# A two-layer adjacency network on one core: exponentials ahead of the ramps, x added in the second layer, the weight splits moved off GpSimd, the packed codes three tiles ahead

## What is computed

```python
# layer 0: h = relu(layernorm(x)); two attention steps with the same mask
def _gat_layer(h, adj_mask, W_l, lw, lb, a):
    Wh = h @ W_l
    L1, L2 = (lw[:C], lw[C:])
    u = Wh @ L1 @ a
    v = Wh @ L2 @ a
    c = lb @ a
    e = jax.nn.leaky_relu(u + v.T + c, negative_slope=ALPHA)
    scores = jnp.where(adj_mask, e, NEG_INF)
    att = jax.nn.softmax(scores, axis=1)
    return jax.nn.elu(att @ Wh)
h = ALPHA * x + (1.0 - ALPHA) * _gat_layer(h, mask, W[i], lin_w[i], lin_b[i], attn[i])   # i = 0, 1
x = x + concatenate([h0, h1, h2]) @ mlp_w + mlp_b
# layer 1: h = relu(layernorm(x))
a = (adj == 1); x1 = a @ h / sum(a, axis=1)
x = x + concatenate([x1, h]) @ weight + bias
```

## Time and profile before

| what | value |
|---|---|
| median of 3 runs | 1790.13 us (1787.9 to 1791.51) |
| the profiled execution, its own time | 1792.32 us |
| its span, first to last instruction | 1790.5 us |
| busy: PE, DVE, ACT, POOL | 1545.7, 1565.8, 1249.3, 144.9 us |
| mean granted TensorE clock | 0.962 of full |
| HBM read and written | 323.35 MB and 27.33 MB |

### The profile page before, as it was taken

The page is one execution under the profiler, slowest core; times in us unless marked ns, Lnnn a source line. Parts: engine busy times, 40 slices in busy tenths (PEclk is TensorE's granted clock), DMA queues, the critical chain, the costliest instruction groups (busy, mean ns, idle before and its releaser), DMA issues. The chain is left out here.

```text
span 1790.5 us, 50269 instructions
## 1 busy us (share of the span) xinstructions
PE 1545.7 (86%) x21779; PEld 1495.5 (84%) x21779; DVE 1565.8 (87%) x2551; ACT 1249.3 (70%) x1341; POOL 144.9 (8%) x164
## 2 busy tenths in 40 slices
PE   2247698888888888888959999999999999799998
PEld 1237688788787878887849999999999999799998
DVE  7689999999999999999989859688696888986675
ACT  3266589898888888888768999999999996000000
POOL 1370000010101010101051000000000000000000
PEclk9668999999999999999979999999999999999999
DMA  7938899999999999999311111111211211133231
GB/s 243 239 144 307 337 362 389 373 380 391 376 405 361 407 367 404 360 407 356 151 43 45 56 44 49 39 59 43 61 55 37 60 31 43 54 102 96 84 96 49
DMA packets 114238, 353.93 MB, mean 198 GB/s; under 512 B 9056, under 2 KB 17248, under 8 KB 114016
## 3 DMA queue, kind: packets, MB, share of 16 engines
q1 hardware_dynamic: 92064, 304.50, 45.5%
q0 software_dynamic: 8512, 27.33, 5.7%
q10 hardware_dynamic: 13440, 18.88, 2.9%
HBM read 323.35 MB, written 27.33 MB: 196 GB/s over the span
## 5 line engine op out<-in xcount | busy, mean ns | idle before, releaser
L475 ACT ACTIVATE region<-ub,bigv 128x1024 uint8<-128x1024 f32 x1024 | 1099.3, 1150 | 81.1 <-DMA x_d<-region 30.9
L1445 PE MATMUL bank<-wsplit,region 128*128 128x195 bf16 x8192 | 791.0, 250 | 62.6 <-DVE region L791 53.8
L1445 PEld LDWEIGHTS bank<-wsplit,region 128*128 128x128 fp8e3 x8192 | 696.6, 99 | 76.4 <-DVE region L791 40.5
L1451 PE MATMUL bank<-wsplit,region 128*128 128x130 f16 x8192 | 558.3, 221 | 58.2 <-DVE region L799 56.9
L1451 PEld LDWEIGHTS bank<-wsplit,region 128*128 128x128 fp8e3 x8192 | 500.5, 98 | 87.7 <-DVE region L799 87.4
L799 DVE SCALAR_TENSOR_TENSOR region<-region 128x512 uint32<-128x512 uint32 x512 | 346.0, 694 | 21.7 <-PE bank L1451 21.0
L791 DVE SCALAR_TENSOR_TENSOR region<-region 128x512 uint32<-128x512 uint32 x512 | 343.1, 699 | 1.4 <-ACT region L475 1.3
L811 DVE TENSOR_SCALAR region<-region 128x4096 uint8<-128x4096 int32 x128 | 293.4, 2292 | 0.1
L1660 PE MATMUL bank<-wsplit,region 128*128 128x129 f16 x4096 | 243.3, 222 | 11.1 <-DVE region L1277 11.1
L1660 PEld LDWEIGHTS bank<-wsplit,region 128*128 128x128 fp8e3 x4096 | 241.0, 99 | 12.6 <-DVE region L1277 12.6
L1277 DVE TENSOR_SCALAR region<-region 128x512 uint32<-128x512 uint32 x256 | 100.4, 424 | 42.7 <-PE bank L1660 37.6
(11 more groups left out here) (183 smaller groups left out, 742.8 us busy)
## 6 DMA issues: line engine op xcount, KB each, us to landing
region<-in_adj SPq DMA_DIRECT2D x128, 2048.0 KB, 11.0
region<-codes_d SPq DMA_DIRECT2D x128, 256.0 KB, 2.7
codes_d<-region ACTq DMA_DIRECT2D x64, 256.0 KB, 6.3
ub<-u_d POOLq DMA_DIRECT2D x16, 512.0 KB, 5.8
hg<-h_d POOLq DMA_DIRECT2D x16, 256.0 KB, 4.8
region<-in_x SPq DMA_DIRECT2D x4, 512.0 KB, 6.3
h_d<-wsplit POOLq DMA_DIRECT2D x4, 512.0 KB, 4.3
x_d<-region POOLq DMA_DIRECT2D x8, 256.0 KB, 16.0
```

Source lines behind the costliest of these rows:

```text
L475: last = nc.scalar.activation(sv[:, b, :], ub[G % 2][:, :], ACT.Relu, bias=bigv[l][:, t:t + 1], scale=BIG)
L1445: return nc.tensor.matmul(acc_on[it], columns(onb[U % NS], it, b), wsplit[:, c * TC + 2 * q + b, 0:WC], start=(c == 0 and q == 0 and b == ...
L1451: return nc.tensor.matmul(acc_off[it], columns(offb[U % NO], it, b), woff[:, c * TC + 2 * q + b, WO:WO + WF], start=(c == 0 and q == 0 and ...
```

## The change

1. ScalarE runs `exps(0)` before any ramp of layer 0. The sum with x is no longer made at the start: L631 goes, ScalarE instead writes the MLP product alone (`m0`) next to hw. It lies over the last two on-buffers and the off-buffers, so the first ramps do not wait for its stores, but ramp 6 and the first off-mask do. The eight stores go out from SyncE's queue, between the loads of `adj`. x is read again in layer 1, and `old_x` has one addition more.
2. `split_off` and GpSimd's part go. Blocks 0 of both layers, and block 1 of layer 1, are split wholly on VectorE (`split`, 8 instructions). The other blocks are made by 5 VectorE instructions (`split_scaled`, `split_rest`, `split_last`) and 3 ScalarE casts (`cast_high`, `cast_middle`), spread over the tile ahead.
3. Codes are packed three tiles ahead instead of two, with four code buffers, and the second pair is packed in place in the strided `code` buffer.
4. The weights that the attention vectors don't need are loaded from ScalarE's queue, and VectorE and TensorE start on the six that they do need.
5. At the end of layer 0 `columns_out` of the last group but one and the third on-mask stand later in VectorE's order.

```diff
-NA, NP, NS, NO = 3, 3, 8, 6
+NA, NP, NS, NO = 3, 4, 8, 6
...
-        highp = at(58 * KB, 2 * KB, U8)
-        xb = [packed, highp]
-        pt = [at(60 * KB + 2 * i * KB, 2 * KB, U8) for i in range(NP)]
+        pt = [at(58 * KB + 2 * i * KB, 2 * KB, U8) for i in range(NP)]
...
-        xr = at(66 * KB, 16 * KB, FP32).rearrange("p (t c) -> p t c", c=C)
+        xq = [at(78 * KB + 4 * ((k + 1) % 4) * KB, 4 * KB, FP32).rearrange("p (t c) -> p t c", c=C) for k in range(4)]
+        m0 = [at(78 * KB + 2 * ((k + 2) % 8) * KB, 2 * KB, FP32).rearrange("p (t c) -> p t c", c=C) for k in range(NG)]
...
+        STORES = {3: (0,), 4: (1, 2), 5: (3,), 6: (4, 5, 6, 7)}
+
+        def nth(l, c):
+
+            return c if l == 0 else NCH - 2 + c
 
...
                     if m >= NA:
                         sp.wait_ge(coded, m - NA + 1)
                     sp.dma_start(adjb[m % NA], adj_v[g, h, :, :, c * CHJ:(c + 1) * CHJ]).then_inc(adj_in[m % NA], 16)
+                    for k in STORES.get(m, ()):
+                        sp.wait_ge(mm_out, 3 * k + 3)
+                        sp.dma_start(dgrp(m0_d, k), m0[k]).then_inc(m0_st, 16)
...
-                def split_off(l, c):
...
-                    ch.step(nc.gpsimd.tensor_tensor(po[:, 0:n, :], hw[:, ts, :], expv[:, ts, 1:2].to_broadcast([P, n, CE]), ALU.mult))
-                    ch.step(nc.gpsimd.tensor_copy(hi, po[:, 0:n, :]))
-                    nc.gpsimd.tensor_tensor(lo, po[:, 0:n, :], hi, ALU.subtract).then_inc(w_off, 1)
-                    pool.wait_ge(w_off, NCH * l + c + 1)
...
-                    pool.wait_ge(x0_r, 3 * k + 3)
-                    pool.dma_start(dgrp(x0_d, k), xr[:, grp(k), :]).then_inc(x0_st, 16)
...
                         pool.wait_ge(xm_r, e)
-                    pool.dma_start(xg[0], dgrp(x0_d, e)).then_inc(xg_in[0], 16)
+                    pool.dma_start(pairs(xi[e % 2]), xin_v[e]).then_inc(xi_in[e % 2], 16)
...
-                        nc.scalar.activation(hw[:, t0:t0 + nt, 0:C], pv[:, :, 0:C], ACT.Copy, scale=winv).then_inc(mm_out, 1)
+                        nc.scalar.activation(hw[:, t0:t0 + nt, 0:C], pv[:, :, 0:C], ACT.Copy, scale=winv)
+                        nc.scalar.activation(m0[X][:, 3 * r:3 * r + nt, :], pv[:, :, C + 2:], ACT.Copy, scale=winv).then_inc(mm_out, 1)
...
-                    elif U == 0:
-                        act.wait_ge(x0_st, 16 * NG)
+                    elif U == NS - 2:
+                        act.wait_ge(m0_st, 16 * NG)
...
+                def cast_high(l, c):
+                    act.wait_ge(sp_a, 2 * nth(l, c))
+                    nc.scalar.activation(wsplit[:, grp(c), 0:CE], av[:, :, :], ACT.Copy)
+                    nc.scalar.activation(woff[:, grp(c), WO:WO + CE], po[:, :, :], ACT.Copy).then_inc(sp_h, 1)
+
+                def cast_middle(l, c):
+                    act.wait_ge(sp_b, nth(l, c))
+                    nc.scalar.activation(wsplit[:, grp(c), CE:2 * CE], bb[:, :, :], ACT.Copy).then_inc(sp_m, 1)
...
+                    rows = slice(C * hf, C * (hf + 1))
+                    act.dma_start(wcat[rows, 0:3 * HC].rearrange("c (l x) -> c l x", x=HC)[:, :, C + 2:HC],
...
+                act.dma_start(mlpb[:, :], mlp_b.partition_broadcast(P)).then_inc(wts, 16)
+                act.dma_start(b1b[:, :], bias1.partition_broadcast(P)).then_inc(wts, 16)
...
                             products(k - 1, r, bank[3 * ((k - 1) % 2) + r])
-                ramps(0, 0, 0)
+                take_codes(0)
+                store_codes(0)
                 exps(0)
...
                     g, r = n // NCH, n % NCH
-                    if n > 0:
-                        ramps(0, n, 0)
+                    ramps(0, n, 0)
+                    if g == 0 and r > 0:
+                        cast_high(0, r)
                     ramps(0, n, 1)
-                    take_codes(n)
+                    if n + 1 < NT:
+                        take_codes(n + 1)
                     if r == 5 and g > 0:
                         high(NG + g - 1)
                     ramps(0, n, 2)
-                    store_codes(n)
+                    if n + 1 < NT:
+                        store_codes(n + 1)
+                    if g == 0 and r > 0:
+                        cast_middle(0, r)
                     ramps(0, n, 3)
                     if g > 0 and r == 7:
...
+                        if g == 0 and r > 1 and q == 0:
+                            cast_high(1, r)
+                        if g == 0 and r > 1 and q == 2:
+                            cast_middle(1, r)
...
                                             ALU.mult).then_inc(u_r, 1)
-                    nc.vector.scalar_tensor_tensor(xr[:, t0:t0 + nt, :], pv[:, :, C + 2:], winv, xr[:, t0:t0 + nt, :],
...
-                def split_on(l, c):
+                def split(l, c):
...
+                    sc.mark(nc.vector.tensor_tensor(full, hw[:, ts, :], expv[:, ts, 0:1].to_broadcast([P, n, CE]), ALU.mult))
+                    sc.mark(nc.vector.tensor_tensor(small, hw[:, ts, :], expv[:, ts, 1:2].to_broadcast([P, n, CE]), ALU.mult))
+                    sc.sync()
+                    sc.mark(nc.vector.tensor_copy(part[0], full))
+                    sc.mark(nc.vector.tensor_copy(hi, small))
+                    sc.sync()
+                    sc.mark(nc.vector.tensor_tensor(rest, full, part[0], ALU.subtract))
+                    nc.vector.tensor_tensor(lo, small, hi, ALU.subtract).then_inc(w_off, 1)
+                    sc.sync()
                     sc.step(nc.vector.tensor_copy(part[1], rest))
                     nc.vector.tensor_tensor(part[2], rest, part[1], ALU.subtract).then_inc(w_on, 1)
...
+                def split_scaled(l, c):
+                    dve.wait_ge(w_on, NCH * l + c)
+                    dve.wait_ge(w_off, NCH * l + c)
+                    nc.vector.tensor_tensor(av[:, :, :], hw[:, grp(c), :], expv[:, grp(c), 0:1].to_broadcast([P, IT, CE]), ALU.mult).then_inc(sp_a, 1)
+                    nc.vector.tensor_tensor(po[:, :, :], hw[:, grp(c), :], expv[:, grp(c), 1:2].to_broadcast([P, IT, CE]), ALU.mult).then_inc(sp_a, 1)
+
+                def split_rest(l, c):
+                    dve.wait_ge(sp_h, nth(l, c))
+                    nc.vector.tensor_tensor(bb[:, :, :], av[:, :, :], wsplit[:, grp(c), 0:CE], ALU.subtract).then_inc(sp_b, 1)
+                    nc.vector.tensor_tensor(woff[:, grp(c), WO + CE:WO + WF], po[:, :, :], woff[:, grp(c), WO:WO + CE],
+                                            ALU.subtract).then_inc(w_off, 1)
+
+                def split_last(l, c):
+                    dve.wait_ge(sp_m, nth(l, c))
+                    nc.vector.tensor_tensor(wsplit[:, grp(c), 2 * CE:WC], bb[:, :, :], wsplit[:, grp(c), CE:2 * CE],
+                                            ALU.subtract).then_inc(w_on, 1)
 
...
+                    elif U == 0:
+                        dve.wait_ge(m0_st, 16 * NG)
...
                     if n > 0:
-                        dve.wait_ge(pairs_r, 2 * n)
+                        dve.wait_ge(packed_r, n)
...
                     nc.vector.scalar_tensor_tensor(pk, cq[1], 2, cq[0], ALU.logical_shift_left, ALU.bitwise_or).then_inc(pairs_r, 1)
-                    nc.vector.scalar_tensor_tensor(hp, cq[3], 2, cq[2], ALU.logical_shift_left, ALU.bitwise_or).then_inc(pairs_r, 1)
+                    nc.vector.scalar_tensor_tensor(cq[2], cq[3], 2, cq[2], ALU.logical_shift_left, ALU.bitwise_or).then_inc(pairs_r, 1)
 
...
+                    nc.vector.scalar_tensor_tensor(pk, cq[2], 4, pk, ALU.logical_shift_left, ALU.bitwise_or).then_inc(packed_r, 1)
 
...
+                    if k == 4:
+                        convert(1, 0)
                     if k == 5:
-                        convert(1, 0)
+                        convert(1, 1)
                 biased_0()
                 largest_0(NG - 1)
                 max_parts(0)
-                convert(1, 1)
                 max_row(1)
                 pack_pairs(1)
                 max_out(1, hmx[:, 1, :])
                 scales(0)
                 pack(1)
+                convert(2, 0)
                 scales_end(0)
                 split_first(0)
-                split_on(0, 0)
+                split(0, 0)
+                convert(2, 1)
+                pack_pairs(2)
+                pack(2)
...
-                    ahead = n + 2 < NT
+                    ahead = n + 3 < NT
                     dve.wait_ge(p_in, n + 1)
+                    if n + 1 < NCH:
+                        split_scaled(0, n + 1)
                     on_mask(0, n, 0)
                     on_mask(0, n, 1)
                     off_mask(0, n, 0)
+                    if n + 1 < NCH:
+                        split_rest(0, n + 1)
                     if ahead:
-                        convert(n + 2, 0)
...
-                        split_on(0, r + 1)
+                        pack(n + 3)
+                    if n + 1 < NCH:
+                        split_last(0, n + 1)
...
-                columns_out(NG + e - 1)
```

(21 more changed lines are left out.)

97 lines of the change are left out of this document (40 added, 57 removed).

## The result

| | kernel before | changed kernel |
|---|---|---|
| median of 4 runs, us | 1789.59 (1787.9 to 1791.51) | 1757.6 (1757.12 to 1758.86) |
| profiled execution: span, own time, us | 1790.5, 1792.3 | 1755.5, 1757.3 |

A forecast was written before the change was run, and what follows sets the result against it. VectorE was taken to bound layer 0's middle, TensorE 950.2 to 1521.9, VectorE again to 1584.0. Terms 27.6 + 1.6 + 0.7 + 7 - 0.7 = 36.2 us off 1792.3 gave 1756.1, less 2.2 us 1753.9, so 1754; range 1743 to 1770.

The forecast's parts named there:

- Before the first off-mask: Start of layer 0: first off-mask at 90.5 instead of 104.3, set by the last store of m0; 13.8 us gained.
- Tiles 0 and 1: First off-mask to tile 2's first on-mask: 26.2 us instead of 40.0 with GpSimd idle; 13.8 us gained.
- Three tiles ahead: End of layer 0: tile 61 has no conversion left and runs at TensorE's pace, 9.4 us; 1.6 us gained.
- Between the layers: columns_out of group 6 moves behind exp_arg, where ScalarE's exponential hides three quarters of it; 0.7 us gained.
- Start of layer 1: First nine TensorE units: 10.5 us to win with VectorE undisturbed, 3.5 taken back; 7 us gained, bounds 2 and 11.
- the part taken back for ScalarE: Layer 1, tiles 2 to 7: ScalarE 10.2 us per tile against TensorE's 9.1, 6.6 lag, lead about 3; 3.5 us lost.
- Tail: After TensorE's full stretch: old_x(7) has one addition more where VectorE sets the pace; 0.7 us lost.
- the correction of 2.2 us: Whole kernel: profiled execution ran 2.2 us above the median of 1790.1, so 1756.1 became 1753.9.
- the late stores: Rival, start of layer 0: m0 stores land late, off-mask at 97 instead of 90.5, 6.5 us lost, 1760.5; chance 0.15.
- The casts: Rival, start of layer 1: casts bind ScalarE and through it TensorE, nothing gained there, 1761; chance 0.08.
- GpSimd as the cause: Tiles 0 and 1, start of layer 1; rival: slowness not GpSimd's doing, 13.8 and 7 us go, 1775; chance 0.04.
- the strided packing: Rival, 58 tiles of layer 0: packing in place doubles two instructions, 1.2 us more per tile, 1824; chance 0.04.

The follow-up runs named there:

- experiment 3: Changed kernel with codes packed two tiles ahead, as before, instead of three: 1761.52 us, ratio 0.9810 to the kernel before.
- experiment 7: Kernel before with exponentials ahead of the first ramp and stores of u for groups 2 to 7 behind GpSimd's eight splits: 1773.92 us, ratio 0.9879.
- Experiment 4: Changed kernel with GpSimd's stores of u for groups 2 to 7 issued only after 12 off-masks: 1753.53 us, ratio 0.9762 to the kernel before.
- experiment 2: Changed kernel with off-side splits back on GpSimd, on-side ones on VectorE, no casts on ScalarE: 1779.64 us, ratio 0.9913 to the kernel before.
- experiment 8: Three kernels, the changed kernel plus useless GpSimd instructions of various kinds, sizes and tiles; the first took 1797.89 us, no total is given for the others.
- experiment 5: Changed kernel with the eight stores of m0 issued in GpSimd's queue instead of SyncE's: 1761.09 us, ratio 0.9817 to the kernel before.
- c_loop: Changed kernel with stores of u for groups 2 to 7 after 12 off-masks and first conversions one group earlier: 1752.33 us, ratio 0.9766 to the kernel before.

## Why the forecast was near

**Before the first off-mask (13.8 forecast, 11.4 measured).** The early weights gave their 3.2 us (the attention vectors at 14.72 instead of 17.95; this part was not undone alone), and ScalarE paced the loop as said. The term that was off is the last store of m0, taken at 90.5 and landed at 92.9, and the step behind it is "the transfers as a whole start 2 to 3 us sooner with the same bytes". Load 6 did go out early, at 60.0, but took 30.4 us. I also took the waits for loads 3, 4 and 5 at nothing, 9.6 us in all; idle time of VectorE in front of a conversion was one of my own signs of being wrong. These waits hardly show in the time, because the off-mask waited for the stores in any case: VectorE was ready for it at 91.4, 1.5 us before they landed, and in experiment 3 it was ready at 78.6 and gained nothing. Bytes were the wrong measure: the earlier trace rows show loads of 22.9 and 24.6 us, and I read them as a full queue where the small pieces of u stood in front (experiment 7 shows it for the kernel before as well). Experiment 4 prices it: without them the off-mask is at 85.8, still with a wait of 3.25 us for load 3; I had put VectorE's own pace at "by about 88".

**Tiles 0 and 1 (13.8, 12.4).** The mechanism is shown by experiments 2 and 8. The size is off by a count: ten split instructions stand between the two points, not eight, because `split_scaled` of block 3 already stands ahead of tile 2's first on-mask; 27.5 us instead of 26.2.

**Three tiles ahead (1.6).** Measured 1.6 by experiment 3, and 1.7 in the trace (24.3 at tile 61, 26.0 at the last sums). **Between the layers (0.7)**: 0.35, from the last sums to layer 1's first product 23.92 us instead of 24.27 (read from the trace, not undone alone).

**Start of layer 1 (7, measured 9.5).** Up to the ninth unit behind the first the gain is 10.8 us (32.9 against 22.1), as the 10.5 of the forecast. What was mis-sized is the part taken back for ScalarE, 3.5 us. ScalarE was full (30.75 of 33 us, and 12.0 of 12.0 from 913 to 925), but TensorE waited only twice, for an on-mask behind a split that had waited 0.97 us for ScalarE's cast:

```profile
939.06 1.51 PE L1501 MATMUL bank<-wsplit,region 128*128 128x195 bf16 x16 [0.66 <-DVE region L828]
948.97 1.51 PE L1501 MATMUL bank<-wsplit,region 128*128 128x195 bf16 x16 [0.67 <-DVE region L828]
```

That is 1.3 us, which takes the 10.8 to 9.5. ScalarE's period was 9.9 us per tile (first casts at 900.60, 910.52 and 920.42) and not 10.2; so the lag over six tiles is some 4.8 us by my way of reckoning and not 6.6, and the lead took up 3.5 of it where I gave it about 3.

**Tail (-0.7).** Measured -0.74, from 35.79 to 35.05.

The span fell by 35.0 us where the terms gave 36.2; the errors of -2.4, -1.4 and +2.5 cancel in large part, and 0.5 us came in tiles 2 to 60, which I had at nothing. That the sum came out within 1.2 us is in part luck. The rest of the distance from 1754 to the measured 1757.6 is the correction of 2.2 us that I took off for the profiled execution: the changed kernel's own profiled execution was not above its median. Of the rivals, the late stores came in part, 2.4 us of the 6.5, as a symptom of the small pieces; by experiment 5 another queue for them changes nothing measurable. The casts did bind ScalarE but hardly TensorE. GpSimd as the cause is shown, and the strided packing costs nothing (679 ns).

What the sum hid is how the parts depend on each other. I priced them as if each stood alone. The order alone gave 18 us, by parking GpSimd's work under a wait. With all other parts but the splits on top of it the kernel stood no better, at 15.6 us (experiment 2). Moving the splits off GpSimd gave another 19 us from there, 8.6 in tiles 0 and 1 and 11.3 at the start of layer 1. Of the third tile ahead only the 1.6 us at the end show even then (experiment 3).

## What to carry to other kernels

Read GB/s beside the busy share of the DMA engines: full engines at a third of the usual rate were small pieces here, and the remedy was to move those out of the stretch in which something waits. Whether they then go one at a time or together made no measurable difference (0.9755 and 0.9766). In these runs work on GpSimd beside a full VectorE was not free even where nobody waited for GpSimd; price it as a lengthening of VectorE's own instructions, and look whether a wait covers it now that will be gone afterwards. Undo the parts of a change one at a time before you credit any of them.

## What the hardware showed unexpectedly

**GpSimd and VectorE take turns by whole instructions, once GpSimd is in.** A mask of 0.68 us takes 1.54 beside products and 1.10 beside copies of 520 elements. The Trainium skill, page "SBUF — State Buffer", section "SBUF: two separate sides", says that whichever starts first has the pair of ports that the two share for the whole instruction, while the other blocks; the traces of experiments 2 and 8 agree where the two alternate (1.54, 1.10 and 1.62 us), and do not agree in the rows of the next point, where VectorE's later instructions went ahead of a product that had begun. Instructions with one input are slowed as well: a conversion took 2.70 us instead of 2.28.

**But GpSimd gets in only at a pause.** Where each of VectorE's instructions starts 0.07 to 0.1 us before the last ends, a GpSimd product stood for 45.7 and 21.0 us, at 192 and at 520 elements, until VectorE ran out of work, and VectorE lost nothing. A pause of 0.1 us, made by a wait on VectorE's own last result, let it in, in each of the tiles 2 to 6 of experiment 8. How long a pause must be was not tried.

**Six stores of 4 KB in pieces of 8 bytes slowed all transfers for some 6 to 12 us** (123 GB/s with them in the changed kernel and 41 in c_loop, at a full DMA share, and 408 without). Whether it is the pieces' number or their size was not separated.
